# A band product whose preceding-tile part is stacked: copies by SyncE into one tile, three products in place of four

## The chip, the cores and the metric

One core of a Trainium2 chip runs the kernel. The metric is device time in microseconds (us) of one execution; the kernel before takes 490.43 us, the median of 3 runs (489.68 to 490.91). Engines are named as in the profile: PE is TensorE's matmul stream and PEld its weight loads, DVE is VectorE, ACT is ScalarE, POOL is GpSimd, SP is SyncE, which here only issues DMAs.

## The reference

Four images of 256 channels and 32 x 32 positions pass through a convolutional attention, a memory-band layer and a mixture of experts. The part that the change touches is the band layer; `t` holds 1024 tokens of 256 features for each image:

```python
def _L1_attn_ref(input_data, W1, W2, bias):      # MEM_SIZE = 32
    i = jnp.arange(num_steps)[:, None]; j = jnp.arange(num_steps)[None, :]
    diff = i - j
    memory = jnp.where((diff > 0) & (diff <= 32), diff, 0)      # 1024 x 1024, a band
    h_hatt = jnp.einsum('nm,bmd->bnd', memory, input_data)
    h = jnp.einsum('bnd,de->bne', input_data, W1)
    return h + jnp.einsum('bnd,de->bne', h_hatt, W2) + bias

x = _L0_conv_ref(x, ...)                 # q, k, v projections; softmax over groups of 32; gamma * out + x
t = _to_tokens(x)
t = t + _L1_attn_ref(_ln_t(t), W1, W2, bias)
t = t + _L1_ffn_ref(_ln_t(t), expert_sel, keys, values)         # top 2 of 32 experts
```

A token's row of the band reaches back over the 32 tokens before it. The kernel forms z = u W2 first and then applies the band to z.

## The kernel before

The 4096 tokens are 32 tiles of 128 (`NT` = 32), eight to an image (`TB` = 8). A main loop runs over steps s = 0 to 31; each engine has its own instruction stream, written out by hand, and semaphores order them. A tile passes through stages that lag the step: energies at s = t, `attend` and the first sum at s = t+1 (`S_AV`), `turn` at t+2, `mix` at t+3 (`S_MIX`), `memory` and the second sum at t+4 (`S_NORM2`), then norm, routing and the scatter of rows. After the loop the last tiles are drained by hand, then a plan is made, and groups of rows go through the experts.

On PE a step is, in this order (L1357 to L1400): `energies(s)`, `memory(s-4)`, `second_turn(s-5)`, `attend(s-1)`, `positions(s-6)`, `logits(s-5)`, a q or k projection in two steps of eight, `mix(s-3)`, `v_proj` for the next image up to step 23, `turn(s-2)`.

`mix(t)` leaves u W1 and z in one bank. ScalarE's `z_high` (L680) writes z rounded to fp32r into `z_hi`, VectorE's `z_low` (L870) the remainder into `z_lo`; both tiles hold three tokens tiles in rotation (`t % 3`). `memory(t)` (L1324) adds band times z: two products with the tile's own halves and, unless the tile is the first of an image, two with the halves of tile t-1, whose band block is `band_r[:, P:2P]`. Only the last 32 rows of tile t-1 meet non-zero entries of that block. `second_sum` (L887) then reads the result.

On VectorE a step begins with `v_evac` (L858, of v_proj) and `z_low(s-4)`, then the maximum and subtraction of the energies, the routing's small operations, `second_sum`, `turned_low`, the sums of the exponentials, and near the end `first_sum(s-1)` (L874), which counts up `t1_done`.

SP's queue (L398 to L415) runs over t: it waits for `t1_done` of t-3 counts, that is for `first_sum(t-4)`, which is done in step t-3, and loads tile t's rows of x into `xt` (L405). At t = 7, 15 and 23 `spread_k` (L390) follows with sixteen copies of `k_once` into `k_s`, each 32 partitions x 1 KB inside SBUF; at t = 4 and 12 a load of the next image's `xc` follows.

Of the kernel before, what the change touches and what calls it, by code (L numbers as in the profile page):

```python
# [12 lines left out]
F32 = mybir.dt.float32  # L13
F32R = mybir.dt.float32r
# [4 lines left out]
ACT = mybir.ActivationFunctionType  # L19
AX = mybir.AxisListType  # L20

P = 128
B, C, H, W = 4, 256, 32, 32
HW = H * W
N = B * HW
TB = HW // P
NT = N // P
# [4 lines left out]
REACH = 32  # L32
# [27 lines left out]
S_AV, S_TURN, S_MIX, S_NORM2, S_ROUTE, S_POS, S_SEND = 1, 2, 3, 4, 5, 6, 7  # L60
LAST = S_SEND
RB = 5
Q_STEP, K_STEP = 2, 3

def attention_moe(nc, x_cm, x_tok, wqk4, bqk4, wvT, bv, gamma, w1, w2, bias, selT, keys, values, out):
    slots_d = nc.dram_tensor("slot_rows", [NE * CAP + P, ROW], F32, kind="Internal").ap()

    with ExitStack() as ctx:
        def sb(name, shape, dt=F32):  # L70
            return ctx.enter_context(nc.sbuf_tensor(name, shape, dt))
# [4 lines left out]
        def sem(name):  # L76
            return ctx.enter_context(nc.semaphore(name))
# [16 lines left out]
        band = sb("band", [P, 2 * P])  # L94
        band_r = sb("band_r", [P, 2 * P], F32R)
# [37 lines left out]
        uT_lo = sb("uT_lo", [P, 2, CH, P], F32R)  # L133
        z_hi = sb("z_hi", [P, 3, C], F32R)
        z_lo = sb("z_lo", [P, 3, C], F32R)
        t2 = sb("t2", [P, NT, C])
        w12 = t2[:, NT - 2 * CH:].rearrange("p (s a) n -> p s a n", s=2)
        w12_as = t2[:, NT - 2 * CH:].rearrange("p (s a) n -> p a s n", s=2)
        mv2 = sb("mv2", [P, 2, 2])
        rstd2 = sb("rstd2", [P, 2, 3])  # L140
        rows = sb("rows", [P, RB, 2, ROW])
        u2T = sb("u2T", [P, 2, CH, P])
# [110 lines left out]
        w_hi_done, w_lo_done, uT_hi_done = sem("w_hi_done"), sem("w_lo_done"), sem("uT_hi_done")  # L253
        uT_mm, uT_lo_done, hz_mm, h_mm, t2_done = sem("uT_mm"), sem("uT_lo_done"), sem("hz_mm"), sem("h_mm"), sem("t2_done")
        band_done, z_hi_done, z_lo_done = sem("band_done"), sem("z_hi_done"), sem("z_lo_done")
        mv2_done, ve2_done, rstd2_done = sem("mv2_done"), sem("ve2_done"), sem("rstd2_done")
        u2_done, u2_copied, u2T_mm, u2T_out = sem("u2_done"), sem("u2_copied"), sem("u2T_mm"), sem("u2T_out")
        lg_mm, ex_done, ex1_done, sig_done = sem("lg_mm"), sem("ex_done"), sem("ex1_done"), sem("sig_done")
# [16 lines left out]
        def after(eng, s, n):  # L275

            if n > 0:
                eng.wait_ge(s, n)
# [43 lines left out]
        def proj_work(s):  # L322

            b, j = s // TB + 1, s % TB
            return (b, j) if s >= 0 and b < B else None

        def k_made(b):

# [29 lines left out]
        def z_at(t):  # L358
            return hz_at(t)[:, C:2 * C]
# [15 lines left out]
        def _(sp):  # L375
# [14 lines left out]
            def spread_k(b):  # L390
                sp.wait_ge(k_out, k_made(b))
                after(sp, e_mm, TB * (b - 1))
                for c in range(WT):
                    for g in range(WT):
                        sp.dma_start(k_s[c * QK:(c + 1) * QK, b % 2, g].rearrange("p j v -> p (j v)"),
                                     k_once[g * QK:(g + 1) * QK, :]).then_inc(k_spread, 16)

            for t in range(NT):  # L398
                if t == 4:
                    sp.dma_start(keys_s[:, :, :, :], keys.rearrange("(a p) e h -> p a e h", p=P)).then_inc(ld_keys, 16)  # L400
                    for side in range(2):
                        sp.dma_start(values_s[side * HID:(side + 1) * HID, :, :], values).then_inc(ld_keys, 16)
                if t >= 4:
                    sp.wait_ge(t1_done, t - 3)
                sp.dma_start(xt[:, t % 4, :], x_tok[t * P:(t + 1) * P, :]).then_inc(ld_xt[t % 4], 16)  # L405
                if t % TB == TB - 1 and t // TB + 1 < B:
                    spread_k(t // TB + 1)
                b = t // TB + 2
                if t % TB == 4 and 2 <= b < B:

                    sp.wait_ge(v_mm, v_no(b - 2, KB - 1) + 1)
                    sp.wait_ge(q_mm, b - 1)
                    sp.wait_ge(k_mm, k_made(b - 2))
                    sp.dma_start(xc[:, b % 2, :, :],
                                 x_cm[:, b * HW:(b + 1) * HW].rearrange(half, p=P)).then_inc(ld_xc[b % 2], 16)  # L415

            sp.wait_ge(const_done, 1)
            sp.dma_start(slots_d[NE * CAP:NE * CAP + P, :], pad_rows[:, 0, :]).then_inc(spare_done, 16)
            sp.wait_ge(spare_done, 16)
# [215 lines left out]
        def _(act):  # L635
            a = nc.scalar
# [43 lines left out]
            def z_high(t):  # L680
                act.wait_ge(hz_mm, t + 1)
                after(act, h_mm, t - 1)
                a.activation(z_hi[:, t % 3], z_at(t), ACT.Copy).then_inc(z_hi_done, 1)

            def second_turned(t):
# [30 lines left out]
            for s in range(NT):  # L716
# [16 lines left out]
                if s == 0:  # L733
                    act.wait_ge(ld_wmix, 48)
                    a.activation(w12_hi[:, :, :, :], w12_as, ACT.Copy).then_inc(w_hi_done, 1)
                    act.wait_ge(const_done, 1)
                    a.activation(band_r[:, :], band[:, :], ACT.Copy).then_inc(band_done, 1)
                work = proj_work(s)
                if work and work[1] == Q_STEP:
# [109 lines left out]
        def _(dve):  # L849
            v = nc.vector  # L850
# [12 lines left out]
                                       op0=ALU.mult, op1=ALU.add).then_inc(v_out, 1)  # L863

            v.memset(warm[:, :], 0.0).then_inc(warm_ready, 1)
            dve.wait_ge(ld_bqk, 16)
            for c in range(2):
                first_k_evac(c)
# [338 lines left out]
        def _(pe):  # L1207
# [116 lines left out]
            def memory(t):  # L1324
                pe.wait_ge(z_lo_done, t + 1)
                pe.wait_ge(band_done, 1)
                sides = [(band_r[:, 0:P], t)] + ([(band_r[:, P:2 * P], t - 1)] if t % TB > 0 else [])
                terms = [(b_, z[:, n % 3, :]) for b_, n in sides for z in (z_hi, z_lo)]
                for i, (b_, z) in enumerate(terms):
                    mm = m.matmul(h_at(t), b_, z, start=False, stop=(i == len(terms) - 1), skip_group_check=True)  # L1330
                mm.then_inc(h_mm, 1)
# [202 lines left out]
```

## Time and profile before

| what | value |
|---|---|
| median of 3 runs | 490.43 us (489.68 to 490.91) |
| span of the profiled execution, first to last instruction | 449.5 us |
| median less that span: what lies around it (the profiled execution's own total isn't given) | 40.9 us |
| PE busy | 379.7 us, 84% |
| DVE busy | 334.4 us, 74% |
| POOL busy | 295.9 us, 66% |
| ACT busy | 277.4 us, 62% |
| share of the ending chain: PE, DVE, issue | 51%, 19%, 9% |

The page is of one execution. Busy shares are averages over stages with different limits: the main loop lies between about 44 and 275 us, the drain and the plan up to about 307 us, the experts after that. A PE that is listed busy is not PE at its peak, since products overlap and their ends are modelled; the distance between the starts of two products tells what one of them takes of the stream. "Idle before" names what ended a wait. The granted clock of TensorE is 1.00 at 2.4 GHz and 0.50 at 1.2 GHz.

### The profile page before, as it was taken

The page shows a single profiled execution, that of the slowest core. Times are in us where ns is not written, and L with a number is a line of the kernel's source. Part 1 is how long each engine was busy: PE and PEld are TensorE (multiplying, and loading weights), DVE is VectorE, ACT ScalarE, POOL GpSimd, SP SyncE. Part 2 cuts the span into 40 slices and gives each one's busy share as a digit, 9 for nine tenths or more (in the row PEclk, how much of TensorE's full clock was granted, in tenths as well). Part 3 has the DMA queues.
Part 4 walks back from the last instruction along what each step waited for, and adds up shares of the span by engine and source line. Part 5 has one row for each costly group of instructions (what it writes and reads, how often), then busy time and mean ns, then how long its engine had stood idle before and what let it go on. Part 6 is the DMA issues. An engine that isn't in the chain of part 4 may idle for free.

```text
span 449.5 us, 10462 instructions
## 1 busy us (share of the span) xinstructions
PE 379.7 (84%) x3007; PEld 291.5 (65%) x3007; DVE 334.4 (74%) x1027; ACT 277.4 (62%) x819; POOL 295.9 (66%) x383
## 2 busy tenths in 40 slices
PE   8989999999999999999999998768799969881000
PEld 3756787876787877787878786525687768771000
DVE  1865788986998986898999995883699988894010
ACT  1243577766677775777778785826599879770000
POOL 6334456775777776777788888763667777777700
PEclk9999999999999999999999999968899989898555
DMA  7999310141121111131121111126888665531297
GB/s 207 365 203 190 103 43 25 51 151 37 52 93 49 48 49 50 49 96 49 37 71 49 62 38 71 61 72 199 255 260 249 180 188 175 157 104 40 85 242 186
DMA packets 31321, 52.73 MB, mean 117 GB/s; under 512 B 7036, under 2 KB 24334, under 8 KB 30765
## 3 DMA queue, kind: packets, MB, share of 16 engines
q1 hardware_dynamic: 23104, 29.48, 24.4%
q0 software_dynamic: 7872, 21.40, 15.0%
q10 hardware_dynamic: 288, 1.18, 0.7%
q8 instruction: 25, 0.41, 0.4%
q14 instruction: 32, 0.26, 0.2%
HBM read 31.56 MB, written 25.73 MB: 127 GB/s over the span
## 4 chain that ended last, share of the span: by engine, by line
PE 51%; DVE 19%; issue 9%; POOL 6%; DMA 6%; ACT 3%; DVEq 2%; SPq 1%; ACTq 0%; POOLq 0%
PE bank L1347 21%; PE bank L1309 9%; PE bank L1238 6%; PE bank L1330 4%; DVE rows L1180 3%; DVE vT L1166 3%; PE bank L1337 3%; DMA out<-vT,dest 3%; POOL out L617 3%; DVE vT L862 2%; DVE z_lo L872 2%; DMA xc_or_xin<-out 2%; POOL slot_rows L520 2%; DVE q_s L1149 1%; PE bank L1220 1%
## 5 line engine op out<-in xcount | busy, mean ns | idle before, releaser
L1347 PE MATMUL bank<-vT,prob 128*128 128x256 f32 x512 | 116.0, 380 | 1.7 <-POOL prob L543 1.7
L1347 PEld LDWEIGHTS bank<-vT,prob 128*128 128x128 f32 x512 | 94.9, 190 | 14.1 <-POOL prob L543 2.3
L617 POOL DMA_INDIRECT out<-vT,dest x80 | 79.6, 996 | 28.4 <-issue 14.9
L520 POOL DMA_INDIRECT slot_rows<-rows,slot x64 | 65.0, 1015 | 16.7 <-issue 15.1
L543 POOL TENSOR_TENSOR prob<-prob,ginv 128x1024 f32<-128x1024 f32 x32 | 61.3, 1914 | 21.0 <-DVE ginv L964 21.0
L514 POOL TENSOR_TENSOR rstd<-rstd,half_neg 128x1 f32<-128x1 f32 x64 | 35.9, 561 | 46.9 <-ACT rstd L667 46.5
L726 ACT ACTIVATE prob<-prob 128x1024 f32<-128x1024 f32 x32 | 33.8, 1057 | 19.6 <-DVE prob L932 19.6
L928 DVE TENSOR_REDUCE gmax<-X 128x32 f32<-128x1024 f32 x32 | 39.2, 1224 | 7.9 <-PE X L1272 7.8
L958 DVE TENSOR_REDUCE gsum<-prob 128x32 f32<-128x1024 f32 x32 | 38.7, 1210 | 3.6 <-ACT prob L726 3.5
L932 DVE TENSOR_TENSOR prob<-X,gmax 128x1024 f32<-128x1024 f32 x32 | 39.2, 1224 | 1.1
L1166 DVE SCALAR_TENSOR_TENSOR vT<-bank,wgt,vT 128x256 f32<-128x256 f32 x80 | 33.2, 477 | 6.7 <-PE bank L1485 5.3
L1180 DVE COPY rows<-values_s 64x256 f32 x112 | 34.4, 307 | 3.6 <-issue 2.4
L1238 PE MATMUL bank<-wv,xc_or_xin 128*128 128x256 f32 x128 | 32.6, 384 | 2.4 <-DVE t L880 2.4
L663 ACT ACTIVATE squares<-t,mv 128x256 f32<-128x256 f32 x64 | 31.7, 495 | 2.2 <-DVE t L880 2.1
L862 DVE SCALAR_TENSOR_TENSOR vT<-bank,gam,gbv 128x256 f32<-128x256 f32 x32 | 14.9, 479 | 24.4 <-PE bank L1238 24.3
L822 ACT ACTIVATE k_s<-keys_s 128x128 f32 x112 | 24.7, 306 | 9.4 <-issue 9.3
L1238 PEld LDWEIGHTS bank<-wv,xc_or_xin 128*128 128x128 f32 x128 | 23.5, 189 | 9.1 <-DVE t L880 3.8
L703 ACT ACTIVATE rows<-t,rstd 128x256 f32<-128x256 f32 x32 | 19.2, 599 | 16.0 <-POOL rstd L516 16.0
L800 ACT ACTIVATE prob<-X 128x512 f32<-128x512 f32 x40 | 21.5, 590 | 11.3 <-PE X L1454 11.2
L807 ACT ACTIVATE vT<-xc_or_xin 128x256 f32<-128x256 f32 x48 | 24.8, 593 | 5.1 <-DMA out<-vT,dest 5.1
L1309 PE MATMUL bank<-w_hi,uT_hi 128*128 128x512 f32 x60 | 26.4, 440 | 0.1
L1466 PE MATMUL X<-prob,k_s 128*128 128x256 f32 x96 | 24.4, 400 | 0.7 <-ACT prob L800 0.7
(205 smaller groups left out, 851.6 us busy)
## 6 DMA issues: line engine op xcount, KB each, us to landing
xc_or_xin<-slot_rows SPq DMA_DIRECT2D x32, 130.0 KB
xt<-x_tok SPq DMA_DIRECT2D x32, 128.0 KB, 2.1
values_s<-values SPq DMA_DIRECT2D x2, 2048.0 KB, 28.5
out<-out POOLq DMA_DIRECT2D x4, 832.0 KB, 14.9
xc_or_xin<-x_cm SPq DMA_DIRECT2D x3, 1024.0 KB, 9.2
t<-slot_rows SPq DMA_DIRECT2D x16, 130.0 KB
t<-slot_rows SPq DMA_DIRECT2D x32, 65.0 KB
xc_or_xin<-slot_rows SPq DMA_DIRECT2D x32, 65.0 KB
```

Of the source, the lines that this page charges most:

```text
L514: g.tensor_tensor(rstd[:, t % 2, 1:2], rstd[:, t % 2, 0:1], half_neg[:, :], ALU.pow).then_inc(rstd_done, 1)
L520: g.indirect_dma_start(out=slots_d, out_offset=bass.IndirectOffsetOnAxis(ap=slot[:, t % RB, r:r + 1], axis=0), in_=rows[:, t % RB, r, :], ...
L543: g.tensor_tensor(prob[:, t % 2], prob[:, t % 2], ginv[:, t % 2].unsqueeze(2).to_broadcast([P, WT * KB, W]), ALU.mult).then_inc(prob_done, 1)
L617: g.indirect_dma_start(out=out, out_offset=bass.IndirectOffsetOnAxis(ap=dest[:, n % (2 * NB), k:k + 1], axis=0), in_=yb[:, n % NB, k, :], ...
L928: v.tensor_reduce(gmax[:, s % 2].rearrange("p (w j) -> p w j", w=WT), E.rearrange("p w (j v) -> p w j v", v=W), AX.X, ALU.max).then_inc(ma ...
L932: v.tensor_tensor(prob[:, s % 2].rearrange("p (j w) v -> p w j v", w=WT), E.rearrange("p w (j v) -> p w j v", v=W), gmax[:, s % 2].rearran ...
L958: v.tensor_reduce(gsum[:, s % 2], prob[:, s % 2], AX.X, ALU.add).then_inc(sum_done, 1)
L1166: v.scalar_tensor_tensor(out=yb[:, n % NB, k, :], in0=Y_p[n % 2][k % 2][:, k // 2, :], scalar=wgt[:, n % (2 * NB), k:k + 1], in1=yb[:, n % ...
L1180: done = v.tensor_copy(into, values_s[side, bass.ds(expert[2 * k + r], 1), :].rearrange("p e n -> p (e n)"))
L1238: mm = m.matmul(dst, x, w, start=(i == 0), stop=(i == len(terms) - 1))
L1309: mm = m.matmul(hz_at(t), u[:, t % 2, a, :], w[:, a].rearrange("p s n -> p (s n)"), start=(i == 0), stop=(i == len(terms) - 1))
L1347: mm = m.matmul(av_p, pr[:, j, :], vT[:, b % 2, j, :], start=(j == 0), stop=(j == KB - 1))
```

## The change

The last 32 rows of `z_hi` and `z_lo` of a tile are copied by two DMAs on SP into one tile, `z_end`: rows 0 to 31 from `z_hi`, rows 32 to 63 from `z_lo`; the other 64 rows are zero from the start. A matching `band_end` holds the block's last 32 rows twice and zeros below. `memory(t)` then multiplies `band_end` by `z_end` once in place of two products with the whole halves of tile t-1. This is done for t-1 from 0 to 27 where t-1 isn't the last of an image, 25 tiles; the last tiles keep the two products. The copies of tile t-7 stand on SP behind the load of `xt` of tile t, those of tiles 25 to 27 behind the loop.

```diff
+END_COPY = 7
+LAST_FULL = 4
+        z_end = sb("z_end", [P, 2, C], F32R)
+        band_end = sb("band_end", [P, P], F32R)
+        def end_copied(t):
+            return 0 <= t < NT - LAST_FULL and t % TB < TB - 1
+        def ends_copied(t):
+            return len([n for n in range(t % 2, t + 1, 2) if end_copied(n)])
 # sync
+            def copy_end(t):
+                sp.wait_ge(z_lo_done, t + 1)
+                after(sp, h_mm, t)
+                for part, z in enumerate((z_hi, z_lo)):
+                    sp.dma_start(z_end[part * REACH:(part + 1) * REACH, t % 2, :].bitcast(F32),
+                                 z[P - REACH:P, t % 3, :].bitcast(F32)).then_inc(z_ended[t % 2], 16)
                 sp.dma_start(xt[:, t % 4, :], x_tok[t * P:(t + 1) * P, :]).then_inc(ld_xt[t % 4], 16)
+                if end_copied(t - END_COPY):
+                    copy_end(t - END_COPY)
                 if t % TB == TB - 1 and t // TB + 1 < B:
                     spread_k(t // TB + 1)
 ...
+            for t in range(NT - END_COPY, NT):
+                if end_copied(t):
+                    copy_end(t)
 # scalar
                 after(act, h_mm, t - 1)
+                if end_copied(t - 3):
+                    act.wait_ge(z_ended[(t - 3) % 2], 32 * ends_copied(t - 3))
                 a.activation(z_hi[:, t % 3], z_at(t), ACT.Copy).then_inc(z_hi_done, 1)
 ...
+                    for side in range(2):
+                        a.activation(band_end[side * REACH:(side + 1) * REACH, :], band[P - REACH:P, P:2 * P], ACT.Copy)
                     a.activation(band_r[:, :], band[:, :], ACT.Copy).then_inc(band_done, 1)
 # vector
+            v.memset(z_end[2 * REACH:P, :, :].bitcast(F32), 0.0)
+            v.memset(band_end[2 * REACH:P, :].bitcast(F32), 0.0).then_inc(end_clear, 1)
 # tensor
-                sides = [(band_r[:, 0:P], t)] + ([(band_r[:, P:2 * P], t - 1)] if t % TB > 0 else [])
-                terms = [(b_, z[:, n % 3, :]) for b_, n in sides for z in (z_hi, z_lo)]
+                terms = [(band_r[:, 0:P], z[:, t % 3, :]) for z in (z_hi, z_lo)]
+                if end_copied(t - 1):
+                    pe.wait_ge(end_clear, 1)
+                    pe.wait_ge(z_ended[(t - 1) % 2], 32 * ends_copied(t - 1))
+                    terms.append((band_end[:, :], z_end[:, (t - 1) % 2, :]))
+                elif t % TB > 0:
+                    terms += [(band_r[:, P:2 * P], z[:, (t - 1) % 3, :]) for z in (z_hi, z_lo)]
                 for i, (b_, z) in enumerate(terms):
                     mm = m.matmul(h_at(t), b_, z, start=False, stop=(i == len(terms) - 1), skip_group_check=True)
```

## Rows read from the trace of the kernel before

**Rows 1.** Stage table: stretch, length, each engine's busy us (instructions), granted clock, DMA
```profile
140.00:160.00 20.00, 19.91 (x166) 16.23 (x165) 17.97 (x60) 14.57 (x45) 15.03 (x20) 1.00 0.16 55
```

**Rows 2.** Chain of waits, pieces in several steps: start us, length us, what
```profile
153.15 0.34 DVE z_lo L872
...
153.53 0.74 PE bank L1330 x4
...
154.49 3.46 PE bank L1347 x16
...
161.68 0.74 PE bank L1330 x4
...
220.86 0.74 PE bank L1330 x4
...
228.18 0.74 PE bank L1330 x4
```

**Rows 3.** Timeline of PE at `memory`: start us, length us, instruction
```profile
153.76 0.28 PE L1330 MATMUL bank<-z_lo,band_r 128*128 128x256 f32 x1
...
154.11 0.38 PE L1321 MATMUL bank<-ident,rows 128*128 128x128 f32 x2
```

**Rows 4.** Timeline of DVE: the last instruction of four first sums
```profile
118.67 0.08 DVE L880 DVE_READ_ACCUMULATOR t<-bank,xt 128x1 f32 x1
...
151.21 0.09 DVE L880 DVE_READ_ACCUMULATOR t<-bank,xt 128x1 f32 x1
...
159.37 0.08 DVE L880 DVE_READ_ACCUMULATOR t<-bank,xt 128x1 f32 x1
...
219.37 0.08 DVE L880 DVE_READ_ACCUMULATOR t<-bank,xt 128x1 f32 x1
```

**Rows 5.** Timeline of SP's queue around `spread_k`: start us, length us, issues
```profile
61.32 0.58 SPq L405 DMA_DIRECT2D xt<-x_tok  x1
...
119.21 10.04 SPq L395 DMA_DIRECT2D k_s<-k_once  x16
129.29 0.58 SPq L405 DMA_DIRECT2D xt<-x_tok  x1
...
198.09 0.58 SPq L405 DMA_DIRECT2D xt<-x_tok  x1
```

**Rows 6.** Two lines of SP: issue ns min/median/max, and the xt load's landing
```profile
L405 SPq DMA_DIRECT2D xt<-x_tok x32: 327/328/797, 8.5 to 248.6; - x32
...
DMA to landing us min/median/max: 2.0/2.1/20.5
...
L395 SPq DMA_DIRECT2D k_s<-k_once x48: 517/591/1188, 51.2 to 196.9; - x48
```

**Rows 7.** Stage table around the second k copy's bytes; last columns: clock, DMA share, GB/s
```profile
120.80:121.00 0.20, 0.15 (x9) 0.10 (x1) 0.04 (x1) 0.18 (x1) 0.20 (x1) 1.00 0.00 0
121.00:121.30 0.30, 0.30 (x3) 0.30 (x4) 0.26 (x1) 0.00 (x0) 0.30 (x1) 1.00 0.40 109
121.30:121.60 0.30, 0.30 (x5) 0.30 (x5) 0.30 (x1) 0.00 (x0) 0.20 (x2) 1.00 0.00 0
```

**Rows 8.** Timeline of PE: first product of `memory` for tiles 2, 10, 18
```profile
60.91 0.39 PE L1330 MATMUL bank<-z_hi,band_r 128*128 128x256 f32 x1
...
129.05 0.38 PE L1330 MATMUL bank<-z_hi,band_r 128*128 128x256 f32 x1
...
197.26 0.38 PE L1330 MATMUL bank<-z_hi,band_r 128*128 128x256 f32 x1
```

**Rows 9.** Timeline of PE after a pause, and the stage table behind it
```profile
365.41 0.84 PE L1454 MATMUL X<-ident,t 128*128 128x128 f32 x6 [1.88 <-ACT prob L800]
...
367.80:371.20 3.40, 3.40 (x17) 3.31 (x17) 2.11 (x8) 3.40 (x12) 2.79 (x3) 0.50 0.62 190
```

**Rows 10.** Waits of PE from 260 to 290 us: total us, times, longest
```profile
PE bank L1347 <- POOL prob L543: 1.1, 1, 1.1
```

**Rows 11.** Timeline of ACT and DVE at the start; idle us before each in brackets
```profile
22.45 1.06 ACT L726 ACTIVATE prob<-prob 128x1024 f32<-128x1024 f32 x1 [5.17 <-DVE prob L932]
...
7.96 0.75 DVE L854 TENSOR_SCALAR k_s<-bank,bqk 128x512 f32<-128x512 f32 x1 [6.74 <-PE bank L1212]
```

More of the change, by code:

```diff
@@ L255, in attention_moe @@
         band_done, z_hi_done, z_lo_done = sem("band_done"), sem("z_hi_done"), sem("z_lo_done")
+        z_ended, end_clear = [sem(f"z_ended{i}") for i in range(2)], sem("end_clear")
         mv2_done, ve2_done, rstd2_done = sem("mv2_done"), sem("ve2_done"), sem("rstd2_done")
```

## The prediction

> **What bounds the kernel now.** I read the table of stages first. In the main loop (about 44 to 275 us) TensorE is busy 19.9 of 20 us at a granted clock of 1.00, VectorE 18.0 and GpSimd 15.0 [rows 1] (one stage; the others of the loop are alike), so whatever lengthens or shortens PE's instruction stream there moves the end. Next the chain of waits: one step of the loop is 8.15 us while v projections run (153.53 to 161.68) and 7.32 us after step 23 (220.86 to 228.18) [rows 2]. The chain leaves PE only once in a step, for v_evac and z_low on VectorE, comes back at `memory` (L1330), and PE waits there for next to nothing: z_lo ends at 153.49 and the product starts at 153.53 [rows 2]. `memory` therefore stands on the path, and everything on PE behind it (second turn, attend, logits, mix, v_proj, the next energies) shifts with it.
>
> **What is removed.** One of four products, for tiles 1 to 28 except 8, 16, 24: 25 products. Their listed 0.28 us is latency; products overlap. In order of time the second to fourth start 0.35 us before the next instruction in three equal steps, so one is worth 0.12 us of stream [rows 3]. 25 x 0.12 = 2.9 us at best. Taking 0.28 would give 7.0; the spacing is the right reading, since PE is never idle between them.
>
> **What is added on idle engines.** Two memsets on VectorE before the first k evacuation, which follows 6.7 us of idleness, and two 32-partition copies on ScalarE in step 0, ahead of 5.2 us of idleness [rows 11]. Nothing there; were that cover gone, four instructions of at most 0.8 us, the nearest row's size.
>
> **What is added on the path: two copies on SP's queue and a wait on PE.** This decides the case. The new waits stand in `memory` ahead of all three products, so PE holds even the tile's own two products, and all work queued behind them, until the previous tile's tail has landed. When is it issued? `copy_end(t-7)` stands behind the xt load of tile t, which waits for first_sum of tile t-4. That is in the same step in which z_low of tile t-7 was made, so the copy goes out only at that step's very end, and the next step's `memory` wants it. Between the end of first_sum (151.21 + 0.09 = 151.30) and `memory` (153.53) lie 2.23 us; in steps after 23 only 1.41 (219.45 to 220.86) [rows 2, 4].
>
> What the chain needs from the end of first_sum: 0.46 us to the first copy's issue, as in the step in which SP issues xt, passes two waits and begins the k copies (118.75 to 119.21) [rows 4, 5]; then that issue. The k copies have exactly this shape (32 partitions x 1 KB, inside SBUF) and each holds SP for 0.52 to 0.59 us, 16 of them in 10.04 [rows 5, 6]; I take 0.56. Then the second copy, from issue to landing. No row shows that alone. Lower bound: the second k copy is issued near 119.8, its bytes move between 121.0 and 121.3 and none for 0.3 us after, so at least 1.4 us [rows 7]. Upper bound: the xt load, four times the bytes from the same queue, 2.0 at the least and 2.1 in the median [rows 6]; contention with scatters could make it 2.4. I take 1.9, close to xt, because the landing comes after the last byte. With 0.04 to wake PE, as after z_lo [rows 2]: 0.46 + 0.56 + 1.9 + 0.04 = 2.96 us.
>
> The Trainium skill (DMA: Bandwidth & Descriptors, "Anatomy of one DMA — SWDGE (gpsimd) path") gives about 2.0 us plus bytes/436e3 for one DMA, measured on GpSimd's path; for 32 KB that is an estimate of 2.08, against my 1.9 from rows. By it the sum below would be about 1.8 us longer.
>
> **Ordinary steps.** With the saving `memory` would arrive 2.23 - 0.12 = 2.11 us after first_sum; it needs 2.96: a stall of 0.85. First_sum itself does not move with a short stall: it ends 5.92 us after `memory` starts (153.53 to 159.45), while attend ends at 157.95, 1.50 before it [rows 2, 4], and only some 0.45 of that is first_sum's own work. So a stall gives the next copy 0.85 us more, and stalls alternate: one in two tiles. In the steps with q and k projections PE has 1 to 2 us more and none occurs. Stalled: tiles 4, 6, 12, 14, 20, 0.85 each = 4.2. Tiles 21 to 23 arrive after 1.41 - 0.12 + 0.85, hence 0.82 each = 2.5 (the balance repeats). Tile 25 follows an unstalled step: 2.96 - 1.29 = 1.67. Sum 8.4. Copies of tiles 25 to 27 stand behind the loop, gated only by z_low, and land a step early.
>
> **Steps behind spread_k.** At t = 7, 15, 23 SP issues sixteen k copies right behind `copy_end(t-7)`. Before, the next xt load leaves late (61.32, 129.29, 198.09) [rows 5] and nobody cares, since xt is wanted four steps on. Now `copy_end` of tiles 1, 9 and 17 stands behind that load, and `memory` of tiles 2, 10, 18 waits for it; these start at 60.91, 129.05 and 197.26 [rows 8], before the queue is even free. The queue is longer by the two copies ahead (0.56 + 0.59 and some 0.09 of waits = 1.24), then 2.93 from xt's issue to PE (2.96 without the 0.03 before it). 61.32 + 1.24 + 2.93 - 60.91 = 4.58; likewise 4.41 and 5.00. This includes the stall and savings of the tile before (1, 9, 17). Sum 14.0.
>
> **What the waits set off.** PE would stand idle some 3.8 us at once, three times. Later in this trace a pause of 1.88 us on PE, at 363.5, was followed by a granted clock of 0.50 (1.2 GHz) for 3.4 us from 367.8 on [rows 9] (one of three such places). Half speed for 3.4 busy us loses 1.7; if part of it falls into the stall, less. I take 1.3 each: 3.9, bounds 0 and 5.1. Against this, GpSimd sets the end near 270 (attend of tile 31 waits 1.1 us for `prob` of L543) [rows 10], and PE's delays let it get ahead; of the 1.1 I give back 0.5 (bounds 0 and 1.1). ScalarE's new wait in z_high for the copy of tile t-3 costs nothing: PE has waited for that copy one step earlier. The xt, xc and k copies move back 1.2 us on SP and are wanted steps later.
>
> **The sum.** 8.4 + 14.0 - 19 x 0.12 (the 25 tiles without the six inside the spread steps' figures: 2.3) - 0.5 + 3.9 = +23.5 us. The page's span is 449.5; the median is 490.43, the 40.9 around the span staying as they are. 490.43 + 23.5 = 513.9 us. Landing time is the strongest lever: 0.1 us changes about ten stalls by 0.1, so 1.4 us gives 508.9 and 2.4 gives 518.9.
>
> **Rivals.** (1) The same stalls, but the clock stays at 1.00, because PE is dense on both sides of each stall, unlike in [rows 9]: 510.0. (2) Copies land late, 2.4 us and more, among scatters of GpSimd or stray late packets, and long stalls reach VectorE through second_sum, so that alternation fails: 519 to 526. (3) On the other side: the copies are there in time. Then only the saving is left, 490.4 - 2.9 = 487.5. It decides at a copy that lands within 1.1 us of its issue; and k copies must not hold the queue. Bytes that first move 1.2 us after issue [rows 7] and a queue that frees after `memory` is due [rows 5, 8] speak against it. (4) SP's hold of 0.56 is only back-pressure of sixteen copies in a row, and lone copies issue in 0.33 like xt [rows 6]: the first lets the second go 0.23 sooner, in the ten stalls 2.3, and the pair ahead of each spread saves 0.5, another 1.5: 3.8 less, 510.1, or 506.2 without the clock's loss. (5) The stalls are absorbed by slack that I don't see and only the removal counts against them: within 0.3% of 490.4.
>
> **How the numbers follow.** Forecast 0.50, rival 1 0.20, rival 2 0.12, rival 3 0.05, rival 4 0.10, rival 5 0.03. The likeliest gives 513.9. The range must leave out no more than 2 in 10: it leaves out rivals 3 and 5 and the far part of rival 2: 505 to 521. About 0.3% (1.5 us) is what a measurement of this kernel can tell from no change: faster 0.05, same 0.03, slower 0.92.
>
> **What would show it.** In the changed trace PE's idleness before L1330's line, now ended by a z_end copy on SP: about 4 us at three places a spread of k copies behind, 0.8 at every other tile, 0.8 at each of tiles 21 to 23, 1.7 at tile 25, none at 26 to 28. Spacing of the three products still 0.12. Copy issue 0.56, landing near 1.9. Granted clock 0.50 shortly after each of the long stalls. I am wrong if L1330's releaser stays z_lo, if copies land in under 1.1 us, or if the main loop keeps its 8.15 us steps.

## The result: 43 us slower, and the profile after

| | before | after |
|---|---|---|
| median of six runs | 490.12 us (487.72 to 491.43) | 537.53 us (529.36 to 542.07) |
| ratio, with its 95% interval | 1 | 1.088 (1.0838 to 1.0921) |
| span of the page | 449.5 us | 530.4 us |

The ratio leaves out the three slowest runs of the changed kernel (539 to 542 us), which ran in a slower state; it puts it at 1.088 x 490.12 = 533 us, 43 us slower. The page of after is of an execution of 532.28 us in all.

The two pages differ by 81 us, which is more than 43. The 449.5 of the page of before is no typical execution: a second profile of the same kernel (first experiment) has a span of 489.2 us in a time of 490.97. Up to the plan's first product (`ident` times `sched`) the two executions of before agree to 0.9 us, once the 1.8 us by which the second starts its loop later are taken off; behind it the page of before takes 148.1 us to its end, the second profile 185.1, after 184.0. So the change is read up to the plan's product, and there the page of before serves. Timelines of PE, of before and of after (columns: start us, length us, engine, line, operation, tiles; in brackets the idle time before it in us and what ended it):

```profile
301.39 0.27 PE L1439 MATMUL bank<-ident,sched 128*4 128x128 f32 x1 [1.56 <-DVE sched L1102]
```
```profile
346.44 0.38 PE L1475 MATMUL bank<-ident,sched 128*4 128x128 f32 x2 [1.66 <-DVE sched L1133]
```

That is 45.05 us later, while the first `memory` starts at 44.73 in before and 44.82 in after (against the second profile of before, where this product starts at 304.10, it is 42.3, close to the 43 of the times). The whole loss lies ahead of the plan, and all but 0.3 us of it in the main loop, as the ledger below shows.

The table of stages over the stretch of [rows 1], in the page of after (columns: stretch, length, busy us and instructions of PE, PEld, DVE, ACT, POOL, granted clock, DMA share, GB/s):

```profile
140.00:160.00 20.00, 14.46 (x127) 11.55 (x126) 12.33 (x38) 9.63 (x30) 11.09 (x14) 0.91 0.17 51
```

PE was busy 19.91 of these 20 us before and is busy 14.46 now, and part of that at half clock. The table of PE's waits names what it waits for (columns: total us, times, longest):

```profile
PE bank L1366 <- DMA z_end<-z_lo: 38.5, 22, 5.2
```

L1366 is `memory`'s product, L1330 before, where PE waited for next to nothing [rows 2]. PE's timeline around three of the 22 waits, the one behind the first `spread_k` (tile 2) and the next two:

```profile
65.49 0.55 PE L1366 MATMUL bank<-z_hi,band_r 128*128 128x256 f32 x1 [4.14 <-DMA z_end<-z_lo]
...
66.69 5.89 PE L1383 MATMUL bank<-vT,prob 128*128 128x256 f32 x16
...
77.12 0.36 PE L1366 MATMUL bank<-z_hi,band_r 128*128 128x256 f32 x1 [0.83 <-DMA z_end<-z_lo]
77.31 0.28 PE L1366 MATMUL bank<-z_lo,band_r 128*128 128x256 f32 x1
77.43 0.28 PE L1366 MATMUL bank<-z_end,band_end 128*128 128x256 f32 x1
77.55 0.38 PE L1352 MATMUL bank<-ident,rows 128*128 128x128 f32 x2
...
86.88 0.36 PE L1366 MATMUL bank<-z_hi,band_r 128*128 128x256 f32 x1 [1.81 <-DMA z_end<-z_lo]
```

Three things are to be seen. The tile's own two products (z_hi, z_lo) are held as well, since the wait stands ahead of all three. The second and third product and the next instruction start 0.12 us apart, as in [rows 3]: the replaced product was worth 0.12. And `attend` (L1383) takes 5.89 us behind the long wait, 3.46 elsewhere, as the clock has fallen in the wait and stays there for nearly the whole of it (same columns as the stage table above):

```profile
61.40:65.50 4.10, 0.01 (x1) 0.04 (x1) 2.77 (x4) 0.01 (x1) 1.31 (x3) 0.87 0.26 72
...
68.00:71.30 3.30, 3.30 (x9) 2.67 (x8) 1.22 (x1) 2.21 (x7) 0.82 (x2) 0.50 0.00 0
71.30:76.30 5.00, 4.98 (x56) 3.65 (x54) 2.28 (x10) 2.36 (x9) 2.06 (x2) 1.00 0.11 33
```

**The ledger.** For each tile I took the time from one start of `memory` to the next in both traces; the growth is a stall on L1366 (less the 0.04 us that PE idled there before), a stretch at clock 0.50, or what is left, the saving. Against the terms of the prediction:

| term | predicted us | in the trace us |
|---|---|---|
| stalls of single tiles, by a landing of 1.9 us | 8.4 | 15.2 |
| stalls of single tiles, what late landings add | 0 | 5.8 |
| tiles 1 and 2, 9 and 10, 17 and 18, saving inside | 14.0 | 15.7 |
| clock at 0.50 | 3.9 (three times) | 10.8 (six times) |
| saving | -2.3 | -2.8 |
| behind the last tile, GpSimd's give-back | -0.5 | +0.3 |
| sum | +23.5 | +45.0 |

The 15.2 are ten tiles at 0.85 (3 to 6, 11 to 14, 19, 20) and four at 1.67 (21, 22, 23, 25), the prediction's own sizes; where the copy landed in 1.9 us they measure 0.78 to 0.84 and 1.61 to 2.09. All single stalls, with the few tenths of tiles 8, 16, 24, 26 and 27, measure 21.0 together, so 5.8 are left for the late ones. Tiles 7 and 15 are wholly among these: a copy that lands in 1.9 us is there before their z_lo, and where theirs is (tile 7 in the last experiment, tile 15 in the one with idle products) they wait for nothing.

### The profile page after: what moved, and what is told of

It is laid out like the page before. It is cut to its first block, busy times and chain, and to the rows that moved or that the text cites. A ratio compares the mean times of both kernels' runs of the same rounds, so it can differ in the third digit from the quotient of the medians.

```text
span 530.4 us, 10512 instructions
## 1 busy us (share of the span) xinstructions
PE 398.9 (75%) x2979; PEld 305.9 (58%) x2982; DVE 339.5 (64%) x1029; ACT 275.8 (52%) x821; POOL 295.6 (56%) x383
## 4 chain that ended last, share of the span: by engine, by line
PE 31%; SPq 20%; issue 15%; DVE 11%; DMA 11%; POOL 4%; another core or an unknown queue 2%; ACT 2%; DVEq 1%; POOLq 0%; ACTq 0%
PE bank L1383 16%; DMA z_end<-z_lo 8%; SPq L408 6%; SPq L461 5%; SPq L464 3%; PE bank L1366 3%; SPq L415 2%; PE bank L1373 2%; PE bank L1269 2%; DVE rows L1211 2%; SPq L287 2%; SPq L425 2%; PE bank L1340 1%; DMA xc_or_xin<-out 1%
## 5 line engine op out<-in xcount | busy, mean ns | idle before, releaser
L1383 PE MATMUL bank<-vT,prob 128*128 128x256 f32 x512 | 123.7, 397 | 1.9 <-POOL prob L568 1.9
L642 POOL DMA_INDIRECT out<-vT,dest x80 | 78.5, 981 | 64.6 <-DVE vT L1197 44.7
L1383 PEld LDWEIGHTS bank<-vT,prob 128*128 128x128 f32 x512 | 101.0, 202 | 16.5 <-POOL prob L568 2.5
L989 DVE TENSOR_REDUCE gsum<-prob 128x32 f32<-128x1024 f32 x32 | 39.0, 1217 | 19.6 <-ACT prob L753 19.1
L715 ACT ACTIVATE u2T<-bank 128x256 f32<-128x256 f32 x31 | 11.9, 382 | 57.4 <-PE bank L1352 54.7
L1366 PE MATMUL bank<-z_hi,band_r 128*128 128x256 f32 x31 | 12.3, 397 | 39.0 <-DMA z_end<-z_lo 38.5
L753 ACT ACTIVATE prob<-prob 128x1024 f32<-128x1024 f32 x32 | 33.5, 1047 | 13.3 <-DVE prob L963 13.3
L1211 DVE COPY rows<-values_s 64x256 f32 x112 | 37.4, 334 | 3.9 <-issue 2.6
L1366 PEld LDWEIGHTS bank<-z_hi,band_r 128*128 128x128 f32 x31 | 6.3, 202 | 51.9 <-issue 36.4
L851 ACT ACTIVATE k_s<-keys_s 128x128 f32 x112 | 24.5, 299 | 10.1 <-issue 10.1
L1502 PE MATMUL X<-prob,k_s 128*128 128x256 f32 x96 | 28.0, 443 | 1.1 <-ACT prob L829 0.7
L1490 PE MATMUL X<-ident,xc_or_xin 128*128 128x128 f32 x96 | 14.2, 295 | 19.4 <-DMA xc_or_xin<-slot_rows 11.6
```

The lines of the kernel that those rows point to most:

```text
L642: g.indirect_dma_start(out=out, out_offset=bass.IndirectOffsetOnAxis(ap=dest[:, n % (2 * NB), k:k + 1], axis=0), in_=yb[:, n % NB, k, :], ...
L753: a.activation(prob[:, s % 2], prob[:, s % 2], ACT.Exp).then_inc(exp_done, 1)
L989: v.tensor_reduce(gsum[:, s % 2], prob[:, s % 2], AX.X, ALU.add).then_inc(sum_done, 1)
L1211: done = v.tensor_copy(into, values_s[side, bass.ds(expert[2 * k + r], 1), :].rearrange("p e n -> p (e n)"))
L1383: mm = m.matmul(av_p, pr[:, j, :], vT[:, b % 2, j, :], start=(j == 0), stop=(j == KB - 1))
```

## Which wait moves which: the chain of waits of after

The prediction let every other stall fall away, because `first_sum` would not move with a stall. The chain of waits over one whole step (columns: start us, length us, what) shows that it does:

```profile
83.90 2.85 DMA z_end<-z_lo
...
86.88 0.59 PE bank L1366 x3
...
87.69 3.46 PE bank L1383 x16
...
91.19 0.47 PE bank L1373 x4
...
91.68 0.21 ACT ex L720
...
91.91 0.04 DVE ex L992
...
92.01 0.07 DVE ginv L995
...
92.27 0.39 DVE t L911 x2
...
92.68 0.33 SPq L425
...
93.11 0.51 SPq L415
...
93.66 1.88 DMA z_end<-z_lo
...
95.67 0.60 PE bank L1366 x3
```

Read from the top: a copy lands, `memory` runs, then second turn, `attend`, positions, and the `logits` of another tile (L1373). ScalarE takes their exponential (L720), VectorE adds one to it (L992, called ex1), and only behind that, in VectorE's queue, stand the reciprocal (L995) and `first_sum` (L911), though neither needs ex1. `first_sum` releases SP: xt, the two copies, and the next `memory` waits for the second of them. It is a closed ring. VectorE's timeline shows the wait inside it, and that it is of another tile's routing:

```profile
91.91 0.18 DVE L992 TENSOR_SCALAR ex<-ex 128x32 f32<-128x32 f32 x1 [0.63 <-ACT ex L720]
```

So each stall moves the next copy by itself, and every step stalls anew by the same amount. What the copy needs was rightly sized: from the end of `first_sum` (92.66) to the product (95.67) it is 3.01 us, against the predicted 2.96.

## The experiments

Theory A: the loss is all waiting. The copies are issued at the step's end, `first_sum` carries each stall on through ex1, the sixteen k copies make three long stalls, and pauses bring the clock down. Rivals: (B) the copies cost by themselves (SP's queue, traffic, ports); (C) the stacked product is no cheaper; (D) what is lost in a single step is only late landing, not the ring. Plan times below are the start of the plan's first product on PE, which is 301.39 in the page of before and 346.44 in after.

**The kernel before, once more.** Nothing is edited.

> The kernel before, unchanged, for a second profile beside the first. Between the plan's product (L1439) and the end the first profile has 148 us (301.4 to 449.5), the changed kernel's 184 us (346.4 to 530.4), though nothing there was changed. If that part simply has two lengths in either kernel, this run shows the plan's product again near 301 us and 180 to 190 us behind it (total near 490). If the first profile is typical for this kernel, the part is 148 us again and the total near 451, and then the changed kernel's later part was lengthened by the change.

Measured 490.97 us, span 489.2. The plan's product is at 304.10. Its first `memory` is at 46.5, 1.8 us later than in the page of before; so the loops agree to 0.9 us. From there to the end it takes 185.1 us instead of 148.1. The 37 us between the two pages of one kernel lie in the experts, and none of them belongs to the change.

**The stacked product without the copies.** All 50 copies and every wait for them are left out (the diff shows the main parts); the stacked product reads zeros, so the result lacks the preceding tile's part.

```diff
-                if end_copied(t - END_COPY):
-                    copy_end(t - END_COPY)
...
-                    pe.wait_ge(z_ended[(t - 1) % 2], 32 * ends_copied(t - 1))
...
-            v.memset(z_end[2 * REACH:P, :, :].bitcast(F32), 0.0)
+            v.memset(z_end[:, :, :].bitcast(F32), 0.0)
```

> The changed kernel without the 50 copies and without every wait for them; the stacked product stays and reads a tile of zeros, so the preceding tile's part is left out of the result. Theory (a product is worth 0.12 us of PE's stream, the rest of the loss is waiting for copies): the plan's product comes 25 x 0.12 = 2.9 us earlier than before, near 298.5, and the total is 0.6% below before. Rival (a product is worth its listed 0.28 us): 7 us earlier. Rival (the stacked product or its weight tile is itself slow): not earlier than 301.4.

Measured 486.38 us, ratio 0.9918 (0.9888 to 0.9948). The plan is at 299.54, 1.9 earlier than in the page of before. Two starts of `memory` on PE:

```profile
60.44 0.39 PE L1358 MATMUL bank<-z_hi,band_r 128*128 128x256 f32 x1
68.47 0.39 PE L1358 MATMUL bank<-z_hi,band_r 128*128 128x256 f32 x1
```

A step is 8.03 us, where before it is 8.15: 0.12 for a product, as predicted, and C falls. Up to the product of tile 23 the loop gains 2.5 us, but the plan only 1.9: the last five stacked products bring nothing. PE waits there for others: 1.39 us for `prob` of GpSimd (1.07 and 1.32 in the two profiles of before [rows 10]) and 0.61 in three waits for z_lo (none and 0.33). All that the idea can bring with this order of work is about 2 us.

**The copies without a reader.** Four products as before; the copies go out, and SP waits for the earlier copy of the same half.

```diff
             def copy_end(t):
+                after(sp, z_ended[t % 2], 32 * (ends_copied(t) - 1))
...
-                if end_copied(t - 1):
-                    pe.wait_ge(end_clear, 1)
-                    pe.wait_ge(z_ended[(t - 1) % 2], 32 * ends_copied(t - 1))
-                    terms.append((band_end[:, :], z_end[:, (t - 1) % 2, :]))
-                elif t % TB > 0:
+                if t % TB > 0:
```

> The kernel before with the 50 copies on SP as in the change, but PE makes its four products and never waits for a copy. Theory (the copies cost only through PE's wait): same as before within 0.3%, plan's product near 301.4, steps of 8.15 us. Rival (the copies themselves disturb SP's queue, the DMA engines or the memory so that other work is late): the plan's product is later by 10 us or more, toward the changed kernel's 346.

Measured 489.06 us, ratio 0.9989 (0.9959 to 1.002); plan at 301.63, 0.24 from before. Fifty copies on SP, late xt loads and all their traffic cost nothing that shows: B falls. What costs is that PE waits for them.

**The copies ahead of the wait for `first_sum`.** The two lines move up on SP, ahead of the wait for `t1_done` and the xt load, so that a copy is gated by its own `z_low` alone.

```diff
+                if end_copied(t - END_COPY):
+                    copy_end(t - END_COPY)
                 if t >= 4:
                     sp.wait_ge(t1_done, t - 3)
                 sp.dma_start(xt[:, t % 4, :], x_tok[t * P:(t + 1) * P, :]).then_inc(ld_xt[t % 4], 16)
-                if end_copied(t - END_COPY):
-                    copy_end(t - END_COPY)
```

> The changed kernel with one thing moved: on SP the copies of tile t-7 stand ahead of tile t's xt load and its wait, so that they go out when z_low is done, some 7 us before the product. Theory (lateness comes from the place behind first_sum, and in three steps from the sixteen k copies ahead in SP's queue): the ordinary stalls vanish, three stalls of 3.4 to 3.7 us stay at tiles 2, 10 and 18, each with a drop of the clock worth 1.4 to 2.8 us; with 2.3 us saved the plan's product comes near 301.4 + 10.5 + 5.5 - 2.3 = 315, total about 3% above before. Rival (DMA landing is slow wherever the copies stand, by contention with scatters): stalls of 0.5 us and more stay in most steps and the plan's product is later than 325.

Measured 503.82 us, ratio 1.0281 (1.0204 to 1.0358), plan at 315.38. Only the three tiles behind a `spread_k` still stall on a copy (3.14, 3.44, 3.31 us); the first of them and the next two tiles:

```profile
63.40 0.55 PE L1366 MATMUL bank<-z_hi,band_r 128*128 128x256 f32 x1 [3.14 <-DMA z_end<-z_lo]
74.28 0.39 PE L1366 MATMUL bank<-z_hi,band_r 128*128 128x256 f32 x1
82.32 0.38 PE L1366 MATMUL bank<-z_hi,band_r 128*128 128x256 f32 x1
```

74.28 to 82.32 is an undisturbed step of 8.04. 63.40 to 74.28 is 10.88: behind the stall the clock fell to 0.50 for 6.8 us, which alone costs 2.8. With the place in SP's order changed, 31 of the 45 us are gone: the order is the cause.

**The same, and the k copies dealt over three turns.** Six, five and five of the sixteen copies go out at t = 7, 8, 9 (and 15, 23 likewise).

```diff
-            def spread_k(b):
+            def spread_k(b, part):
...
+                for n in range((0, 6, 11)[part], (6, 11, 16)[part]):
+                    c, g = n // WT, n % WT
...
-                if t % TB == TB - 1 and t // TB + 1 < B:
-                    spread_k(t // TB + 1)
+                for part in range(3):
+                    if (t - part) % TB == TB - 1 and 0 < (t - part) // TB + 1 < B:
+                        spread_k((t - part) // TB + 1, part)
```

> The changed kernel with its copies ahead of the xt load on SP, as in the run before, and with each set of sixteen k copies dealt out in 6, 5 and 5 over three turns of SP's loop. Theory (only late landing cost anything): no stall at the band products, no clock drop in the main loop, plan's product 2.9 us before 301.5, near 298.6 to 299.5 as in the run without copies, total 0.6% below before. Rival (once the copies are on time something else ends last, or the divided k copies reach energies late): the plan's product at 301 or later, total within 0.3% of before.

Measured 484.35 us beside 486.51 of the kernel before on the same chip, ratio 0.9964 (0.9936 to 0.9991): this version is 0.1 to 0.6% below the kernel before, a small gain but clear of no change. Plan at 299.75, 0.2 from the run without copies, and no stall of L1368 on a copy, so all that the previous experiment left was the block of sixteen. The starts of `memory` for tiles 2 and 3 are 60.73 and 68.77, a step of 8.04.

**The changed kernel with the k copies dealt, the copies where the change puts them.** The edit of `spread_k` just shown, alone.

> The changed kernel with its copies where it has them, and each set of sixteen k copies dealt out over three turns of SP's loop. Theory (the long stalls at tiles 2, 10 and 18 come from the k copies ahead in SP's queue): these stalls fall from 4.1 to 5.2 us to the ordinary 0.85 to 1, their clock drops go, and the plan's product comes 15 to 18 us earlier, 328 to 331. Rival (a third of the k copies ahead is still too much, as SP is the busy queue): stalls of 1.5 us and more in the three steps that have k copies, plan's product no earlier than 336.

Measured 514.33 us, ratio 1.0588 (1.0538 to 1.0638), plan at 328.53: 17.9 us of the 45 go with the block of sixteen. The stalls of tiles 2, 10 and 18 are ordinary ones now, 0.89, 1.20 and 0.82:

```profile
62.65 0.36 PE L1368 MATMUL bank<-z_hi,band_r 128*128 128x256 f32 x1 [0.89 <-DMA z_end<-z_lo]
71.45 0.36 PE L1368 MATMUL bank<-z_hi,band_r 128*128 128x256 f32 x1 [0.84 <-DMA z_end<-z_lo]
```

The step between them is 8.80, an ordinary stall on an undisturbed 8.0. 27 us remain without one stall over 2.3 us: single stalls in nearly every step, and what they set off.

**ex1 behind `first_sum`.** On VectorE the wait for the exponential and the addition move behind `first_sum`; nothing else changes. By A that opens the ring, by D it changes nothing.

```diff
-                for t in tiles(s, S_ROUTE):
-                    dve.wait_ge(ex_done, t + 1)
-                    v.tensor_scalar(ex1[:, t % 2], ex[:, t % 2], 1.0, None, ALU.add).then_inc(ex1_done, 1)
...
+                for t in tiles(s, S_ROUTE):
+                    dve.wait_ge(ex_done, t + 1)
+                    v.tensor_scalar(ex1[:, t % 2], ex[:, t % 2], 1.0, None, ALU.add).then_inc(ex1_done, 1)
```

> The changed kernel with one instruction moved on VectorE: the addition that waits for logits' exponential (ex1, L992) stands behind first_sum and not ahead of it. Theory (a stall of memory reaches first_sum through second_turn, logits, the exponential and ex1, so the next copies are late by the same again and every step stalls): first_sum now keeps its time but for the 0.24 us that come through ScalarE's exp, stalls alternate between about 0.85 and 0.25 us, and the plan's product comes 5 to 8 us earlier than 346.4, at 338 to 341. Rival (first_sum is carried along through ScalarE's queue, second_turned ahead of exp): stalls stay at 0.85 in every step and the plan's product stays within 2 us of 346.4.

Measured 524.33 us, ratio 1.0793 (1.0749 to 1.0836), plan at 338.97, 7.5 earlier than after. Tiles 2 to 5:

```profile
66.00 0.55 PE L1366 MATMUL bank<-z_hi,band_r 128*128 128x256 f32 x1 [4.18 <-DMA z_end<-z_lo]
76.89 0.39 PE L1366 MATMUL bank<-z_hi,band_r 128*128 128x256 f32 x1
86.71 0.36 PE L1366 MATMUL bank<-z_hi,band_r 128*128 128x256 f32 x1 [1.84 <-DMA z_end<-z_lo]
94.82 0.35 PE L1366 MATMUL bank<-z_hi,band_r 128*128 128x256 f32 x1
```

Stalls of tiles 2 to 7 are 4.18, 0.05, 1.84, 0.14, 1.28, 0.63. Tiles 3, 5, 11, 13 and 19, which in after waited 0.82 to 0.88 for copies that landed in 1.9 us, wait 0.05 to 0.21 now: there a stall no longer hands itself on to the next step. One instruction's place in VectorE's queue made the difference, and D falls. The sizes are not the 0.85 and 0.25 that I expected, and the trace shows why.

First, the moved addition has a price. In 16 of its 27 steps it starts while GpSimd's `prob` product runs and takes 1.86 to 1.95 us, in after never over 0.18. z_low stands behind it, and the waits of tiles 6, 9, 14, 17 and 25 to 27 (1.2 to 1.9 us) are for z_lo and for no copy. Timelines of POOL, DVE and PE ahead of tile 6:

```profile
100.42 1.92 POOL L568 TENSOR_TENSOR prob<-prob,ginv 128x1024 f32<-128x1024 f32 x1
100.51 1.86 DVE L1001 TENSOR_SCALAR ex<-ex 128x32 f32<-128x32 f32 x1
104.05 0.38 PE L1366 MATMUL bank<-z_hi,band_r 128*128 128x256 f32 x1 [1.28 <-DVE z_lo L903]
```

Second, there is another way round to `first_sum`. Tiles 21 to 23 still wait about 1.0 us each for their copies; the chain of waits of this run there:

```profile
253.01 0.23 PE bank L1352 x2
...
254.53 1.05 ACT prob L753
...
255.61 1.23 DVE gsum L989
...
257.13 0.38 DVE t L911 x2
```

The second turn (L1352), which stands behind `memory`, lets go ScalarE's copy of it (L715); in ScalarE's queue the exponential of the energies (L753) comes only after that copy, VectorE's sum of the exponentials (L989) waits for it, and `first_sum` (L911) stands behind the sum. No run opened this second ring.

**PE kept at work in the long waits.** Sixteen products on idle data at tiles 2, 10, 18, between the end of the `first_sum` that lets the copies go and the wait.

```diff
+                    if t in (2, 10, 18):
+                        pe.wait_ge(t1_done, t + 3)
+                        for _ in range(16):
+                            m.matmul(bank[7], warm[:, 0:P], warm[:, :], start=True, stop=True)
                     pe.wait_ge(z_ended[(t - 1) % 2], 32 * ends_copied(t - 1))
```

> The changed kernel with sixteen idle products (128x512, into a bank that nobody reads) on PE in the stalls of tiles 2, 10 and 18, ahead of the wait for the copies. Theory (the steps behind the long stalls are longer because the granted clock fell to 0.50): the stalls stay 4 to 5 us, the clock stays 1.00 behind them, the three steps behind are 8.0 to 8.2 us in place of 10.8, 9.6 and 9.4 and the plan's product is some 5.5 us earlier, near 341. Rival (these steps are longer because VectorE and ScalarE are late, whatever the clock): step lengths as before, plan's product near 346.

Measured 519.31 us in the profiled execution (four lie between 516.03 and 524.31), plan at 336.37, 10.1 earlier than after. PE's timeline at tile 2, and the stage table behind the wait:

```profile
61.35 3.63 PE L1364 MATMUL bank<-warm 128*128 128x512 bf16 x16
...
66.17 0.38 PE L1370 MATMUL bank<-z_hi,band_r 128*128 128x256 f32 x1 [1.19 <-DMA z_end<-z_lo]
74.99 0.36 PE L1370 MATMUL bank<-z_hi,band_r 128*128 128x256 f32 x1 [0.84 <-DMA z_end<-z_lo]
```
```profile
66.20:70.00 3.80, 3.80 (x20) 3.44 (x21) 1.39 (x4) 2.96 (x8) 0.00 (x0) 1.00 0.00 0
```

The copy comes no earlier than in after (its product starts at 66.17, there at 65.49), but the clock is 1.00 behind it, and the step is 8.82 us where after takes 11.63 (65.49 to 77.12): the 2.8 us of that step are the clock's, not the stall's. At tile 18 the wait outlasted the idle products and the clock fell all the same. The rest of the 10.1 is a side effect: the stalls of tiles 4, 12 and 20 fell from 1.8 to 0.8 too, and the drops behind tiles 12 and 20 with them. The added instructions had moved the instruction fetches, which the next experiment takes up.

**Instruction fetches moved.** In after, the copies that land in 2.85 us and more, where 1.9 is the rule, lie beside a fetch of instructions on queue q8 (that it is PE's code is inferred from what this experiment moves). The DMA view of the stretch around a late landing in after (columns of a queue: packets, MB, share of 16 engines; of an issue: KB, us to landing), then of a clean one, where q8 has no packet:

```profile
q8 instruction: 1, 0.02, 2.1%
...
z_end<-z_lo SPq DMA_DIRECT2D x1, 32.0 KB, 3.5
```
```profile
z_end<-z_lo SPq DMA_DIRECT2D x1, 32.0 KB, 1.9
```

One packet on q8 with 2.1% of 16 engines over 4.0 us is 1.3 us on one engine. To move these fetches without touching the work, the kernel gets 95 more waits that are already satisfied at the head of PE's stream:

```diff
-            pe.wait_ge(warm_ready, 1)
+            for _ in range(96):
+                pe.wait_ge(warm_ready, 1)
```

> The changed kernel with 95 more waits for a semaphore that is already set at the very start of PE's stream, so that every later instruction of PE lies at another place in its code. Rival (these tiles are late for a reason of the tile, as the scatters or loads beside them): stalls of 1.8 stay at tiles 4, 12 and 20. Total time about that of the changed kernel in either case, within some 5 us.

A single execution: 534.95 us beside 488.88 of before; plan at 349.16, with its loop starting 4 us later. The late landings moved: tile 4 waits 0.81 instead of 1.81, tile 12 0.82 instead of 1.87, tile 20 1.02 instead of 1.86, tile 7 nothing instead of 1.31; but tile 21 waits 3.25 instead of 1.71, with a fetch beside its copy:

```profile
90.19 0.36 PE L1367 MATMUL bank<-z_hi,band_r 128*128 128x256 f32 x1 [0.81 <-DMA z_end<-z_lo]
...
258.59 0.36 PE L1367 MATMUL bank<-z_hi,band_r 128*128 128x256 f32 x1 [3.25 <-DMA z_end<-z_lo]
```
```profile
q8 instruction: 1, 0.02, 2.2%
...
z_end<-z_lo SPq DMA_DIRECT2D x1, 32.0 KB, 3.4
```

So these late landings go with the fetches, not with the tile: in all five traces read for it (after and the last four experiments) every one has a fetch beside it. That the longer code is what moved the fetches, and not chance between two executions, rests on one execution of each. Tile 15 is late again, at 3.2 us, with a fetch beside it. Tile 14, which I had counted among them, has no 16 KB fetch beside its copy in either trace, and it lands in 2.3 and 2.5 us; that one stays open. Why one engine's fetch delays a whole copy (its last bytes, or the write that reports its end) the traces don't show.

## Why the prediction missed

The direction was right (with it rivals 3 and 5 fall), and so was what decides: copies issued at the step's end, and `memory` waiting for them. The size was 23.5 against 45, and the time lies above the range. Of the missing 21.5, the clock has 6.9, the single stalls by the ring 6.8, late landings 5.8 and the steps behind `spread_k` 1.7; the rest is small.

**The product.** Right: 0.12 us, in after (77.31, 77.43, 77.55) and without copies (8.15 to 8.03). That without copies the last five bring nothing was not in the sum; it is 0.6 us.

**What a copy needs.** Right: issue 0.51 for the first, landing 1.88, 3.01 us from `first_sum` to the product for 2.96. The Trainium skill's figure for GpSimd's path (DMA: Bandwidth & Descriptors, "Anatomy of one DMA — SWDGE (gpsimd) path") had led to an estimate of 2.08 for the landing; the trace has 1.88 on SP's queue, so the value taken from the xt load was the better one. Rival 4, lone copies issued in 0.33, is wrong: the 25 pairs took 507 to 578 and 590 to 601 ns, in the lines of SP's issues (columns: ns min, median, max, first and last start us):

```profile
L415 SPq DMA_DIRECT2D z_end<-z_hi x25: 507/507/578, 50.9 to 309.4; - x25
L415 SPq DMA_DIRECT2D z_end<-z_lo x25: 590/591/601, 51.5 to 309.9; - x25
```

**"First_sum itself does not move with a short stall."** This step failed. I compared `first_sum` with the `attend` that feeds it, saw 1.5 us between them, and called that slack. I did not ask what stands ahead of it in VectorE's queue: ex1, which waits for ScalarE, which waits for PE's `logits`, which stand behind `memory`. So fourteen single tiles stall at 0.85 or 1.67 rather than eight at 0.85 or 0.82 and one at 1.67: 15.2 for 8.4. With ex1 moved, the tile behind a stall waited 0.05 to 0.21 in five places, though a second ring through ScalarE kept tiles 21 to 23 at 1.0. Rival 2 had the alternation fail, but through `second_sum` and only where copies are late; the ring needs neither.

**The steps behind `spread_k`.** Right in mechanism: 4.49, 5.35 and 5.87 for 4.58, 4.41 and 5.00, and the first is near. In the other two PE starts 3.47 and 3.34 us after the xt load's issue rather than 2.93; and at the second the k copies begin 0.4 us later than the two copies alone explain, while at the third they take 11.08 us instead of 10.62. The dealt k copies removed these stalls, as the theory wants.

**The clock.** I had three drops at 1.3 us. There were six: at 64.5, 146.4, 166.9, 228.3, 248.8 and 293.2, behind the stalls of tiles 2, 10, 12, 18, 20 and 25. Five lasted 3.4 us and cost some 1.6 each, the first lasted 6.8 and cost 2.8: 10.8 for 3.9. Three of the six follow single stalls of 1.87, 1.86 and 2.20 us, two of them long only through a late landing. [rows 9] had shown a pause of 1.88 us with a drop behind it, so such stalls were in reach of the rows; my only single stall near it was the 1.67 of tile 25, and I gave it no drop. Length alone doesn't tell: in the run with the dealt k copies, stalls of 1.79 and 1.84 us had a drop behind them, 2.06 and 2.21 had none. The price was sized low as well: I let part of a drop of 3.4 us fall into the stall, but five drops cost nearly their whole 1.7, and the one at tile 2 lasted twice as long, most of it over `attend`. Rival 1, the clock stays at 1.00, is wrong.

**Late landings.** My bound of 2.4 us came from scatters; 2.85 to 3.5 in after came beside instruction fetches, of which I had not thought. With tile 14, late landings add 5.8 us, and the drops behind tiles 12 and 20 went with them when those tiles' copies came clean.

**GpSimd's give-back and the 40.9 us around the span.** The 0.5 did not come back (+0.3). And 1.8 us lie around the span (490.97 less 489.2); most of the rest of the 40.9 was a page whose experts ran 33 to 39 us shorter than in the ten other profiles (148.1 for 181.2 to 187.2). What lies around the span is alike with and without the change, so the forecast did not suffer from it, but the sentence was wrong.

Of what was to show it, the releaser at L1366, the spacing, the issue and the clean landing came as written; "0.8 at every other tile" did not: 0.8 at nearly every tile, and 1.7 instead of 0.8 at tiles 21 to 23.

## What to carry to other kernels

Before a stall is written off as absorbed, follow it once around: from the stalled engine through everything queued behind it to each engine that waits, and there to what stands behind that wait in the same in-order queue, needed or not. If the path comes back to the instruction that starts the late transfer, every step pays. A copy that PE is to wait for belongs ahead of unrelated waits and away from blocks of copies in its queue, and a change that is worth 0.12 us a step is measured first without its transfers, as the most that it can bring.

## What the runs showed of the hardware

**A fetch of instructions delays a copy.** A 16 KB fetch (q8) beside the late copies of after holds one DMA engine for 0.9 to 1.3 us, and a 32 KB copy under way beside it landed after 2.85 to 3.5 us instead of 1.9 (up to 3.6 with the dealt k copies). Every z_end landing over 2.6 us that a product waited for, in after and the last four experiments, lies beside one; adding waits that never block to one engine's stream changed which tile paid.

**A VectorE addition beside GpSimd's product.** In the run with ex1 moved, a 128x32 addition on VectorE that starts while GpSimd's 128x1024 `prob` product runs ends within 0.05 us of that product's end: 1.86 to 1.95 us in 16 cases, for 0.18 where it starts ahead of it. What holds it was not tried.

**SP's register instructions in the experts.** In the page of before the moves for the dynamic loads take 29 to 37 ns. In every other profile, with or without the change, 31 to 39 of SP's register instructions there take over 0.3 us, most about 0.7, 21 to 27 us in all, and PE waits longer for the loads behind them (11.2 us in the second profile of before, 3.5 in the page). The line of SP for these moves in the page of before and in the second profile of before (ns min, median, max, first and last start us); in after it reads 3, 29 and 796 ns:

```profile
L439 SPq MOVE t<-slot_rows x32: 29/29/37, 343.7 to 367.6; - x32
```
```profile
L439 SPq MOVE t<-slot_rows x32: 4/29/1431, 358.6 to 398.3; - x32
```

What makes them long was not tried and stays open. If all of it counts it is most of the 37 us between the two pages of before, which isn't shown; the clock also stood at 0.50 for 73.6 us behind the plan in the second profile and for 51.0 in the page. It is a reason to take a second profile of a kernel before a span is subtracted from a time.
